# Gated cross-attention and ternary FFN on one core: token work in 28 tiles of 128 rows, an opening order of its own, casts and layernorm on ScalarE

## What is computed

```python
# x (32,112,256), ctx (32,375,256)
xn = layernorm(ctx, ln1_w, ln1_b)
ln = layernorm(_layernorm(x), ln2_w, ln2_b)
q  = ln @ Wq                              # 256 x 1024
k, v = split(xn @ Wkv)                    # 256 x 2048
q  = q * (1 + s[:, None, :, None]) + s[:, None, :, None]     # s = fside, a factor per head
attn = softmax(einsum('bihd,bjhd->bhij', q, k) / 8)
x  = x + tanh(g_xattn) * (einsum('bhij,bjhd->bihd', attn, v).reshape(b, -1, 1024) @ Wout)
h  = gelu(bitlinear(_layernorm(x), w1, b1))     # act_quant(rmsnorm(.)) @ ternary(w1).T + b1
x  = x + tanh(g_ffn) * bitlinear(h, w2, b2)
```

## Time and profile before

| | |
|---|---|
| median of 3 runs | 1238.8 us (1238.38 to 1241.94) |
| the profiled execution's own time | 1237.77 us |
| its span, first to last instruction | 1235.6 us |
| PE busy | 1131.4 us, 92% |
| DVE busy | 1044.9 us, 85% |
| ACT busy | 855.1 us, 69% |
| POOL busy | 875.2 us, 71% |

### The profile page before, as it was taken

One profiled execution on the slowest core, in us unless ns is written; L12 is line 12 of the kernel. 1 busy time (PEld: TensorE's weight loads), 2 busy tenths in 40 slices (PEclk: granted clock), 3 DMA queues, 4 the chain that ended last, 5 costly groups with the idle time before them and its releaser, 6 DMA issues.

```text
span 1235.6 us, 32509 instructions
## 1 busy us (share of the span) xinstructions
PE 1131.4 (92%) x12354; PEld 768.6 (62%) x12354; DVE 1044.9 (85%) x2224; ACT 855.1 (69%) x1638; POOL 875.2 (71%) x1049
## 2 busy tenths in 40 slices
PE   2778999999999999999999999999999999999964
PEld 1455666666666666667666666766666666666643
DVE  2578898888888898888898888889888888998874
ACT  3455677777777677777777777777777777777742
POOL 4556787777777877777787777778777777877551
PEclk9899999999999999999999999999999999999986
DMA  8245554565555556554646565565655655464440
GB/s 255 44 89 85 99 87 99 102 102 95 109 93 96 91 103 102 97 110 90 104 85 103 100 102 105 93 106 88 100 101 103 98 103 94 87 104 90 85 89 11
DMA packets 381304, 120.48 MB, mean 98 GB/s; under 512 B 354976, under 2 KB 380016, under 8 KB 381152
## 3 DMA queue, kind: packets, MB, share of 16 engines
q1 hardware_dynamic: 381152, 118.42, 53.4%
HBM read 26.63 MB, written 3.67 MB: 25 GB/s over the span
## 4 chain that ended last, share of the span: by engine, by line
PE 44%; DVE 21%; ACT 11%; issue 10%; DVEq 6%; DMA 5%; POOL 3%; POOLq 1%; ACTq 0%
PE work L634 10%; PE work L636 9%; PE work L635 9%; PE ps_s L653 6%; DVE neg_max L561 5%; DMA pt<-pn 4%; DVE pn L568 4%; ACT prob L418 4%; PE ps_o L634 3%; ACT L418 2%; ACT k_h L376 2%; ACT hid_g L428 2%; DVEq L531 2%; DVE k_l L498 2%; PE ps_o L635 2%
## 5 line engine op out<-in xcount | busy, mean ns | idle before, releaser
L271 POOL TENSOR_TENSOR pn<-prob,pn 112x750 f16<-112x750 f32 x256 | 400.3, 1564 | 109.7 <-DVE pn L568 108.6
L418 ACT ACTIVATE prob<-ps_s,neg_max 112x375 f32<-112x375 f32 x512 | 266.0, 571 | 267.8 <-DVE neg_max L561 267.4
L561 DVE TENSOR_REDUCE neg_max<-ps_s 112x2 f32<-112x750 f32 x256 | 238.6, 932 | 17.1 <-PE ps_s L653 17.0
L568 DVE CAST pn<-prob 112x750 f16<-112x750 f32 x256 | 174.6, 682 | 67.0 <-ACT prob L418 66.8
L634 PE MATMUL work<-z,wkv_h 128*128 128x375 f16 x512 | 168.3, 329 | 37.2 <-DVE k_l L498 33.7
L634 PEld LDWEIGHTS ps_o<-v_h,pt 128*128 128x128 f16 (+1 forms) x1536 | 139.7, 97 | 87.9 <-issue 63.9
L634 PE MATMUL ps_o<-v_h,pt 128*128 128x65 f16 (+1 forms) x1536 | 171.8, 197 | 15.7 <-DMA pt<-pn 15.6
L635 PE MATMUL ps_o<-v_l,pt 128*128 128x65 f16 (+1 forms) x1536 | 169.8, 194 | 0.0
L636 PE MATMUL ps_o<-v_h,pt 128*128 128x65 f16 (+1 forms) x1536 | 168.5, 194 | 0.0
L636 PE MATMUL work<-z,wkv_l 128*128 128x375 f16 x512 | 167.1, 326 | 0.0
L635 PE MATMUL work<-z,wkv_h 128*128 128x375 f16 x512 | 166.8, 326 | 0.0
(11 more groups left out here) (131 smaller groups left out, 2924.2 us busy)
## 6 DMA issues: line engine op xcount, KB each, us to landing
ctx_in<-in_ctx SPq DMA_DIRECT2D x32, 375.0 KB
pt<-pn SPq DMA_TRANSPOSE x256, 3.5
x_in<-in_x SPq DMA_DIRECT2D x32, 112.0 KB, 5.7
x_res<-in_x SPq DMA_DIRECT2D x32, 112.0 KB, 2.2
out<-y SPq DMA_DIRECT2D x32, 112.0 KB, 2.6
stage<-in_wkv SPq DMA_DIRECT2D x2, 1024.0 KB, 9.5
stage<-in_w SPq DMA_DIRECT2D x2, 1024.0 KB, 12.2
stage<-in_wq SPq DMA_DIRECT2D x1, 1024.0 KB, 9.3
```

Source lines behind the costliest of these rows:

```text
L271: g.tensor_tensor(pn[p % PBUF][:, 1, :, 0:SK], prob[:, p % 2], pn[p % PBUF][:, 0, :, 0:SK], ALU.subtract).then_inc(p_lo, 1)
L418: i = a.activation(prob[:, p % 2, h, :], ps_s[0:SQ, h, 0:SK], ACT.Exp, bias=neg_max[:, h:h + 1])
L561: v.tensor_reduce(neg_max[:], ps_s[0:SQ, :, 0:SK], X, ALU.max, negate=True).then_inc(max_ready, 1)
L568: v.tensor_copy(pn[p % PBUF][:, 0, :, 0:SK], prob[:, p % 2]).then_inc(p_hi, 1)
```

## The change

The token work after `OO` is no longer done per batch element of 112 rows but per tile of 128 rows of all 3584 tokens, 28 in place of 32. `ot_h` and `ot_l` become a ring of 7 x 128 columns in the dead part of `stage`, and in every eighth iteration the token steps are left out. The layernorm is written by ACT and not by POOL. The casts `PH` of pairs 0, 2, 4, 6 go to ACT, those of 1, 3, 5, 7 stay on DVE. All five tables are new, and each engine has a list `FIRST` for the first two elements, in which the work on weights has steps of its own (`WKH`, `WQH`, `WVH`, `WOH`, `WKL`, `AS0`, `TN0` and so on). The loads of the gates and of the two bias rows move behind the second element's context load; `wkv`'s first half is loaded ahead of the layernorm vectors and `wq` right after them. In the statistics one small DVE operation is saved, and `LNA` has two POOL operations in place of four.

```diff
-SLOTS = PAIRS
+NT = B * SQ // P
+RING = 7 * P
+CAST_ACT = (0, 2, 4, 6)
-PE_ORDER = [
-    ("S0", 0), ("A5", -1), ("V01", 0), ("V02", 0), ("OO0", -1), ("S1", 0), ("A6", -1), ("K0", 1),
...
+ORDER["PE"] = [
+    ("K5", 0), ("K7", 0), ("V00", 0), ("A4", -1), ("S0", 0), ("V01", 0), ("A5", -1), ("V02", 0),
...
+FIRST["PE"] = [
+    ("Z0", 0), ("Z1", 0), ("ZX", 0), ("K0", 0), ("K2", 0), ("K1", 0), ("Q0", 0), ("K4", 0),
+    ("K3", 0), ("K5", 0), ("K6", 0), ("S0", 0), ("Z0", 1), ("V00", 0), ("Z1", 1), ("V01", 0),
...
+START, END = -3, B + 4
+def sequence(engine):
+    done = set(FIRST[engine])
+    steps = FIRST[engine] + [(name, it + off) for it in range(START, END) for name, off in ORDER[engine]
+                             if 0 <= it + off < B and (name, it + off) not in done]
+    return [(name, b - b // 8 - 1 if name in TOKEN_STEPS else b) for name, b in steps if b % 8 or name not in TOKEN_STEPS]
+def last_batch(t):
+    return (t * P + P - 1) // SQ
+def columns(b):
+    return slice(b * SQ % RING, b * SQ % RING + SQ)
+def last_user(b):
+    return [((b - 7) * SQ - 1) // P] if b >= 8 else []
...
-        x1_b2 = stage[0:SQ, 0:B * D]
+        RC = IC * RING // 2
+        ot_h, ot_l = (stage[:, RC * i:RC * (i + 1)].bitcast(F16).rearrange("p (c q) -> p c q", c=IC) for i in range(2))
+        x1_b2 = stage[:, 2 * RC:2 * RC + 4 * D].rearrange("p (s d) -> p s d", s=4)
...
             def split_p(b, p):
-                pool.wait_ge(p_hi, b * PAIRS + p + 1)
+                pool.wait_ge(p_hi_act if p in CAST_ACT else p_hi, CAST_COUNT[b, p])
...
-            def layernorm_write(b):
-                pool.drain()
-                if b > 0:
-                    for n in ("Z0", "Z1", "ZX"):
-                        pool.wait_ge(full[BANK[n, b - 1]], USE[n, b - 1])
-                for t in range(TT):
-                    g.tensor_scalar(ctx_n[:, t, :], ctx_in[:, t, :], ctx_rs[:, t:t + 1], ctx_nb[:, t:t + 1], ALU.mult, ALU.add)
-                g.tensor_scalar(x_n[:], x_in[:], x_rs[:], x_nb[:], ALU.mult, ALU.add).then_inc(ctx_normed, 1)
...
+                if name == "LNW":
+                    act.wait_ge(ln_ready, b + 1)
+                    if b > 0:
+                        for n in ("Z0", "Z1", "ZX"):
+                            act.wait_ge(full[BANK[n, b - 1]], USE[n, b - 1])
+                    for t in range(TT):
+                        a.activation(ctx_n[:, t, :], ctx_in[:, t, :], ACT.Identity, bias=ln_nb[0:TP, t:t + 1], scale=ln_rs[0:TP, t:t + 1])
+                    a.activation(x_n[:], x_in[:], ACT.Identity, bias=ln_nb[0:SQ, TT:TT + 1],
+                                 scale=ln_rs[0:SQ, TT:TT + 1]).then_inc(ctx_normed, 1)
...
+                if name[0:2] == "PH":
+                    p = int(name[2])
+                    g = b * PAIRS + p
+                    act.wait_ge(exp_done, g + 1)
...
+                    if g >= PBUF:
+                        act.wait_ge(turned[p % PBUF], 16 * (g // PBUF))
+                    a.activation(pn[p % PBUF][:, 0, :, 0:SK], prob[:, p % 2], ACT.Identity).then_inc(p_hi_act, 1)
...
                 if name == "WO":
                     if b == 0:
-                        pe.wait_ge(lo_split, 4)
-                    results(b, ["OO0", "OO1"])
-                    i = three(w[0:SQ, 0:D], [(ot_h[:, c, :], ot_l[:, c, :], wout_h[:, c, :], wout_l[:, c, :]) for c in range(IC)])
+                        pe.wait_ge(lo_split[3], 1)
+                    for half in ("OO0", "OO1"):
+                        results(last_batch(b), [half])
+                    r = slice(b % (RING // P) * P, (b % (RING // P) + 1) * P)
+                    i = three(w[:, 0:D], [(ot_h[:, c, r], ot_l[:, c, r], wout_h[:, c, :], wout_l[:, c, :]) for c in range(IC)])
```

More of the change, by code:

```diff
@@ new lines @@
+ORDER["PE"] = [
[6 rows of a table added]
+]
+FIRST["PE"] = [
[11 rows of a table added]
+]
+ORDER["ACT"] = [
[5 rows of a table added]
+]
+FIRST["ACT"] = [
[12 rows of a table added]
+]
+ORDER["DVE"] = [
[6 rows of a table added]
+]
+FIRST["DVE"] = [
[11 rows of a table added]
+]
+ORDER["POOL"] = [
+    ("ZS1", 1), ("PL7", -1), ("XQ", -2), ("PL0", 0), ("QS1", 0), ("LNA", 2), ("PL1", 0), ("PL2", 0),
+    ("XB", -2), ("HQ", -3), ("PL3", 0), ("ZXS", 1), ("PL4", 0), ("PL5", 0), ("RM2", -2), ("RM1", -1),
+    ("QS0", 1), ("ZS0", 2), ("PL6", 0),
+]
+FIRST["POOL"] = [
[5 rows of a table added]
+]
+ORDER["SP"] = [
+    ("ST", -4), ("T6", -1), ("T7", -1), ("RS", -1), ("T0", 0), ("T1", 0), ("T2", 0), ("LD", 3),
+    ("T3", 0), ("T4", 0), ("T5", 0),
+]
@@ L82 @@
+def last_batch(t):
[4 more added lines that the diff above has]
+    return [((b - 7) * SQ - 1) // P] if b >= 8 else []
 BANK, USE = {}, {}
-for n, job in enumerate(j for j in sequence(PE_ORDER) if j[0][0] not in 'SA'):
+for n, job in enumerate(j for j in sequence("PE") if j[0] == "SUM" or j[0][0] not in "SA"):
     BANK[job], USE[job] = n % WORK_BANKS, n // WORK_BANKS + 1
-HI_COUNT = {s: n + 1 for n, s in enumerate(s for s in sequence(ACT_ORDER) if s[0][0:2] in ("KH", "VH"))}
+HI_COUNT = {s: n + 1 for n, s in enumerate(s for s in sequence("ACT") if s[0][0:2] in ("KH", "VH"))}
@@ L88, in build @@
+Q_COUNT = {(s[1], int(s[0][2])): n + 1 for n, s in enumerate(s for s in sequence("POOL") if s[0][0:2] == "QS")}
+CAST_COUNT = {(b, p): sum((i in CAST_ACT) == (p in CAST_ACT) for i in range(PAIRS)) * b
+              + sum((i in CAST_ACT) == (p in CAST_ACT) for i in range(p + 1)) for b in range(B) for p in range(PAIRS)}
 def build(nc, x, ctx, fside, g_x, g_f, ln1w, ln1b, ln2w, ln2b, wq, wkv, wout, w1, b1, w2, b2, out):
@@ L342, in step @@
                     g.tensor_scalar(hid_q[:], hid_r[:], -ROUND, 1.0, ALU.add, ALU.mult).then_inc(hq_ready, 1)
-            for name, b in sequence(POOL_ORDER):
+            for name, b in sequence("POOL"):
                 step(name, b)
@@ L388, in step @@
                     act.wait_ge(full[BANK[job]], USE[job])
-                    a.activation(ot_h[:, 4 * half:4 * half + 4, :], work[:, BANK[job], 0:4 * SQ].rearrange("p (c q) -> p c q", c=4),
-                                 ACT.Identity).then_inc(o_hi, 1)
+                    if b == 0:
+                        act.wait_ge(lo_split[3], 1)
+                    for t in last_user(b):
+                        act.wait_ge(full[BANK["WO", t]], USE["WO", t])
+                    a.activation(ot_h[:, 4 * half:4 * half + 4, columns(b)],
+                                 work[:, BANK[job], 0:4 * SQ].rearrange("p (c q) -> p c q", c=4), ACT.Identity).then_inc(o_hi, 1)
                 if name[0:2] == "QF":
                     half = int(name[2])
+                    if b == 0:
+                        act.wait_ge(side_ready, 1)
                     act.wait_ge(full[BANK[job]], USE[job])
@@ L461, in weight_means @@
             def weight_means():
-                dve.wait_ge(abs_summed, 1)
-                v.tensor_scalar(w_mean[:], ps_o[:, 0, 4 * VW:4 * VW + 2], 1.0 / (FF * D), 1e-5, ALU.mult, ALU.max)
+                bank = BANK["SUM", 0]
+                dve.wait_ge(full[bank], USE["SUM", 0])
+                v.tensor_scalar(w_mean[:], work[:, bank, 0:2], 1.0 / (FF * D), 1e-5, ALU.mult, ALU.max).then_inc(evacuated[bank], 1)
                 dve.drain()
@@ L619, in step @@
                     dve.wait_ge(full[BANK["F2", b]], USE["F2", b])
-                    v.scalar_tensor_tensor(out=y[:], in0=work[0:SQ, BANK["F2", b], 0:D], scalar=deq2t[:], in1=x1_b2[:, bass.ds(b * D, D)],
+                    v.scalar_tensor_tensor(out=y[:], in0=work[:, BANK["F2", b], 0:D], scalar=deq2t[:], in1=x1_b2[:, b % 4, :],
                                            op0=ALU.mult, op1=ALU.add).then_inc(evacuated[BANK["F2", b]], 1)
-            for name, b in sequence(DVE_ORDER):
-                prepare(name, b)
+            for name, b in sequence("DVE"):
                 step(name, b)
```

343 lines of the change are left out of this document (176 added, 167 removed), and 72 rows, old and new, of tables (ACT_ORDER, CAST_ACT, DVE_ORDER, PE_ORDER).

## The result

| | before | changed |
|---|---|---|
| median | 1238.6 us (4 runs beside the changed kernel) | **1169.9 us** (1168.4 to 1170.6, 4 runs) |
| ratio to before, 95% interval | | 0.944 (0.942 to 0.946) |
| span of the profiled execution | 1235.6 us | 1167.3 us |

The kernel is 69 us faster, by 5.6%. Forecast were 42 us and a range that ended at 1179; the direction is right, the size is not. All times compare fast executions; one of the twelve of e9 took 1803 us at a mean granted clock of 0.59 and is left out.

A forecast was written before the change was run, and what follows sets the result against it. PE was taken to bound the middle; 1237.8 us less 18 (tiles), 13 (opening) and 11 (waits) gave 1195.8, plus 1.0 to the median 1196.8 us. The range for 8 in 10 was 1179 to 1225 us.

The forecast's parts named there:

- The tiles: Token steps on PE in the middle: 28 sets for 32, less wider transposes, 18.0 us less.
- one short distance: Sign in the middle: Gelus of neighbouring iterations 34 to 35 us apart, every eighth distance some 5 us shorter.
- The opening up to the first score: PE's waits before the first score shrink: 13 us less, bounds 5 and 20.
- 2.0 us less: Opening: the first K comes this much sooner, with the layernorm writes on ACT and not on POOL.
- 3 + 5.7 = 8.7: Opening: 3 of 4.9 us of PE's waits for DVE saved, and 5.7 us from third-element statistics moved later.
- The slow clock: Opening: with the pause gone, matmuls before the first score no longer run at twice the full-clock spacing, 2 us less.
- Behind the first score: The 16.2 us of PE's idle time there: no term, named only in the opening's bound of 20 us.
- The waits of the middle: PE's 22.3 us of waiting for k_l: 11 us less, bounds 22 us less and 5 us more.
- Half of it: The share of PE's 22.3 us wait in the middle taken as saved, 11 us.
- ScalarE becomes the bound: Rival, middle: ACT at 91% can't keep a shorter period, only the opening's gain remains, 1226 us; chance 0.18.
- Exponentials held up: Rival, middle: casts and layernorm writes on ACT delay exponentials and so the next scores, 1284 us; chance 0.06.
- the opening gains nothing: Rival, opening: a formerly hidden load arrives last, the 13 us fall away, 1210 us; chance 0.10.

The follow-up runs named there:

- e9: The kernel before with one step moved, DVE's subtraction KL5 ahead of the statistics XST: 1239.24 us, ratio 1.000 to before.
- e3: The changed kernel with its token steps on 32 tiles of 112 rows again, all else as changed: 1187.68 us.
- e11: The changed kernel, unaltered, measured again at another time: 1168.45 us, ratio 0.943 to before.
- e6: The changed kernel with the four layernorm writes on POOL again, ahead of the subtraction PL3: 1171.18 us, ratio 0.947 to before.
- e4: The changed kernel with the FIRST opening lists emptied, weight work where the kernel before had it: 1192.27 us.
- e8: The changed kernel, opening lists kept, with only the work on wout, w1 and w2 back at the places of the kernel before: 1177.68 us.
- e7: The kernel before with only the casts of pairs 0, 2, 4, 6 moved to ACT, each behind its exponential: 1264.13 us, ratio 1.022 to before.
- e1: The changed kernel with all eight casts of prob on DVE again, none on ACT: 1185.07 us.

## Why the prediction was right or wrong

**The tiles: right.** 18.0 us forecast, 17.8 by e3 (19.2 against e11), though 15.3 of them in the middle and not all. The saving shows spread over four iterations around each free eighth (33.79, 34.05, 33.36 and 34.64 us instead of 34.97), not as one short distance: the free steps belong to different elements in the order.

**The opening up to the first score: right in sum, by luck.** Forecast 13 us, measured 12.9 in the first profile and 14.2 in that of e11. One step failed and a term that the sum did not have made up for it. The step that failed is "2.0 us less" for the first `K`: it came 1.3 us later. The 2.57 us of POOL's last write, which this step rested on, were not POOL's own time but the contention with DVE's split of `wkv`. The layernorm on ACT did start PE's transposes 2.4 us sooner and POOL's splits of `z` 1.7; but now the two weight splits on DVE lay beside these, and they took 5.8 us in all, where the four had taken 2.8 in before (0.50, 0.90, 0.50 and 0.89). With the writes on POOL again (e6) the first `K` stands at 21.50 us, sooner than with them on ACT (22.22 to 22.48).

Between the first `K` and the first score 14.2 us went, of 10.7 forecast. PE's waits there fell from 11.1 us (1.27, 3.64, 5.70 and one of 0.52) to 2.6 (one of 1.06 left, one of 1.51 for `q_l` new): 8.6 less, for 3 + 5.7 = 8.7 in the sum. The slow clock gives some 2.1 us, an estimate: PE worked 9.7 us of that stretch at the lower level in before and 5.5 now, and half of the difference counts; 2 were forecast. The remaining 3.5 us are the missing term: 67 matmuls stand between the two points, where it was 87, since the new order puts one `K`, one `V` and eight transposes elsewhere. One root was also read wrongly: the wait of 1.27 us came behind DVE's wait for the second element's context (8.58 us, until 24.5 us), not behind constants.

**Behind the first score: costed at nothing, was 13 us.** This is the first large error. The 16.2 us of idle time stood in the earlier trace rows and were named only as a bound. PE's waits of that window would have given 13.2 us for `prob`, and the diff gives the weight steps places of their own: the working stopped at the first score though the opening lists run over two elements. e4 puts 14.7 us on the lists behind the first score, and e8 shows that 9.3 us hang on where the late weight steps stand. The tiles have a part in it too, 3.5 us by e3, which the sum had counted in the middle.

**The waits of the middle: the term was half its size.** 11 us were taken, of a possible 22; PE's idle time there fell by 23.1 us, and against e3 the middle gained 25.6 beside the tiles. "Half of it" had no row behind it. And the bound of 22 counted one wait alone: the DMA waits of 7.8 us in the same went too. The mechanism was also incomplete. The step that failed is that the term hung on DVE's load alone. e9 shows that the wait could not be cured at its place (ratio 1.000), e7 that the relief alone loses 27 us, e1 that the new order with its casts on DVE has more than half of the gain. What worked was both: a new order, and in it the casts on ACT. Which steps of the new order do it stays open. One row was read for what it isn't: the 1.67 us of the earlier trace rows are the duration of one cast, not how long a cast waited for DVE to come round.

**The rivals.** "ScalarE becomes the bound" fell: ACT is at 88% in the middle, and PE waits 1.0 us for `prob`. The Trainium skill ("ScalarE: Activation LUTs", section "Rules for kernel authors") would keep simple arithmetic such as `add` and `mul` on VectorE; casts are not in its list. The measured 839 ns against a median of 554 ns on DVE agree with it per element, but what it advises is e1, 15 us slower here. "Exponentials held up" did not come true in the new tables, nor in the old ones: e7 is slower, at 1264 us, but through high halves that came late and not through exponentials. The rival was priced at 1284 us from half of the added 5.6 us per iteration; e7, with the casts alone, cost 0.97 us per iteration (first scores 36.62 us apart for 35.65). The rival "the opening gains nothing" fell at once.

**The range** ended 9 us above the result. Its lower end held both of the better bounds in full, 1196.8 - 7 - 11 = 1178.8, so the bounds themselves were too narrow. The opening's was 20 us, with what the earlier scores might shorten behind them; it gave 12.9 and 13.3, 26 us (3.5 of them the tiles'). The waits' was 22 us, and 23 to 26 went.

## What to carry to other kernels

A wait on the list can name the place where a circle of engines opens, and not what to mend: move one step and look whether the bound engine's busy time in a fixed window changes (e9: 962 to 963 of 991 us, so no). Where work moves from a full engine to a freer one in strict order, ask which of the freer engine's outputs the full one waits for, and whether they are issued before or behind the new work (the same four casts cost 27 us in the old order, e7, and gained 15 in the new one, e1). Compare the jobs that stand ahead of a milestone before and after, not only the waits there. And take every stretch in which the bound engine is idle as a term of the sum with its own list of waits; what has no term will be costed at nothing.
